# The polar factor of a scan matrix: 20 iterations inside an expert layer instead of 32 inside the attention

## What is computed

```python
x = x + attention(layernorm(x), Wq, bq, Wk, bk, Wv, bv, Wo, bo)
x = x + experts(layernorm(x), Wg, w1, w2)
x = x + scan_block(layernorm(x), W_up, W_v, W_proj, identity, W_scan_raw)
x = x + experts(layernorm(x), Wg, w1, w2)

# inside scan_block: the matrix W of the scan is the polar factor of W_scan_raw (128 x 128)
U, _, Vt = jnp.linalg.svd(W_scan_raw, full_matrices=False)
W = U @ Vt
```

## Time and profile before

| | us |
|---|---|
| three runs | 2096.91, 2099.97, 2100.51 |
| median | 2099.97 |
| the profiled execution | 2098.23 |
| its span | 2096.5 |

### The profile page before, as it was taken

The page is one execution under the profiler, slowest core; times in us unless marked ns, Lnnn a source line. Parts: engine busy times, 40 slices in busy tenths (PEclk is TensorE's granted clock), DMA queues, the critical chain, the costliest instruction groups (busy, mean ns, idle before and its releaser), DMA issues. The chain is left out here.

```text
span 2096.5 us, 44156 instructions
## 1 busy us (share of the span) xinstructions
PE 1715.4 (82%) x14662; PEld 1126.9 (54%) x14662; DVE 1421.2 (68%) x2559; ACT 970.7 (46%) x2157; POOL 688.0 (33%) x498
## 2 busy tenths in 40 slices
PE   5699989998998999899974565899999999994374
PEld 3234333333333433334344554888888888884373
DVE  7777777777787777777624125688888888884222
ACT  4166666776676677676632112233333333332120
POOL 5300000000000000000013432677777777763532
PEclk9599999999999999999965786999999999997587
DMA  3200000000000000000007215122222222212523
GB/s 109 77 17 18 17 11 17 18 17 11 18 17 11 18 17 17 11 17 18 2 21 245 72 46 147 31 81 80 80 80 80 80 80 80 80 50 82 192 69 101
DMA packets 171652, 117.20 MB, mean 56 GB/s; under 512 B 10940, under 2 KB 161852, under 8 KB 171208
## 3 DMA queue, kind: packets, MB, share of 16 engines
q1 hardware_dynamic: 167368, 106.33, 17.3%
q0 software_dynamic: 4096, 8.46, 1.1%
HBM read 63.98 MB, written 50.72 MB: 55 GB/s over the span
## 5 line engine op out<-in xcount | busy, mean ns | idle before, releaser
L557 DVE TENSOR_REDUCE chunk_max<-ps_max 128x1 f32<-128x512 f32 (+3 forms) x1280 | 698.5, 603 | 211.2 <-PE ps_max L663 123.3
L606 ACT ACTIVATE probs<-ps_s 128x512 f32<-128x512 f32 (+3 forms) x1280 | 599.6, 547 | 317.2 <-PE ps_s L655 163.8
L636 PE MATMUL ps_s<-Qs,Ks 50*128 50x512 bf16 (+3 forms) x1280 | 379.3, 357 | 70.7 <-DVE chunk_max L557 50.7
L646 PE MATMUL ps_max<-Ks,Qs 48*128 48x512 bf16 (+3 forms) x1280 | 385.8, 360 | 13.1 <-POOL a_ident L499 10.5
L706 PE MATMUL ps_o<-probs,Vp 128*32 128x512 f32 (+3 forms) x2560 | 349.9, 571 | 11.4 <-ACT O_sb L589 11.1
L514 POOL TENSOR_TENSOR A_b<-A_newton,b_tile 128x128 f32<-128x128 f32 x32 | 14.6, 455 | 917.5 <-ACT A_newton L613 917.5
L1424 POOL TENSOR_TENSOR lane_products<-L,q 128x1024 f32<-128x1024 f32 x132 | 309.5, 2376 | 4.0 <-DMA L<-scanned 4.0
L636 PEld LDWEIGHTS ps_s<-Qs,Ks 50*128 50x128 bf16 x1280 | 103.1, 94 | 311.2 <-DVE chunk_max L557 247.1
L1479 DVE TENSOR_TENSOR weighted<-exp_scores,psV_s 128x4096 f32<-128x4096 f32 x44 | 194.2, 4413 | 0.2 <-issue 0.2
L1437 POOL TENSOR_TENSOR q<-L,z_normed 128x1024 f32<-128x1024 f32 x44 | 141.6, 3218 | 144.7 <-DVE z_normed L1459 144.7
L1558 PE MATMUL psS<-ident,lane_products 128*128 128x128 f32 x1408 | 169.4, 279 | 23.7 <-POOL lane_products L1424 23.7
(11 more groups left out here) (224 smaller groups left out, 2375.0 us busy)
## 6 DMA issues: line engine op xcount, KB each, us to landing
scanned<-q SPq DMA_DIRECT2D x44, 512.0 KB
L<-scanned SPq DMA_DIRECT2D x44, 512.0 KB
m_w<-in_L_ffn_w_dram SPq DMA_DIRECT2D x32, 512.0 KB
Qs<-q_parts SPq DMA_DIRECT2D x192, 32.0 KB
Ks<-k_parts SPq DMA_DIRECT2D x192, 32.0 KB
dispatched<-m_blank SPq DMA_DIRECT2D x2, 2080.0 KB
m_blank<-dispatched SPq DMA_DIRECT2D x16, 260.0 KB
routed<-m_blank SPq DMA_DIRECT2D x2, 2048.0 KB
```

The costliest lines, as they stand in the source:

```text
L557: nc.vector.tensor_reduce(out, scores[:, 0:w], axis=AX.X, op=ALU.max).then_inc(max_reduced, 1)
L606: nc.scalar.activation(dst, ps_s[(k + r) % R][:, q0:], ACT.Exp, scale=SCALE).then_inc(exp_done, 1)
L636: last = nc.tensor.matmul(ps_s[(k + r) % R][:, q0:], K[r][rows, kt * P:(kt + 1) * P], Q[r][rows, g * QW + q0:(g + 1) * QW], start=True, st ...
L646: last = nc.tensor.matmul(ps_max[(k + r) % R][:, 0:w], Q[r][rows, i * P:(i + 1) * P], K[r][rows, ck * QW:ck * QW + w], start=True, stop=no ...
```

## The change

The iteration leaves `attend` altogether: its products, copies and POOL operations, its six tiles, `newton` and two semaphores. `reads` loses the entries "A", "Y" and "X", and the waits that named them name the neighbouring entries. POOL's fill loses `b_tile` and `a_ident`.

`moe` gets an argument `polar`, true for "m0" alone. There 20 iterations run as one chain: 16 with the coefficients SPREAD and 4 with SETTLE (the coefficients used so far). PE runs them between `count(1)` and `turn(0)`, DVE behind `route(1)`, ACT behind `copy_totals(1)`. A and A A lie in the two banks of `psH[0]`, the new S and its transpose in those of `psH[1]`. DVE copies A, makes Z and Y and copies S; ACT copies the transpose. POOL makes the two scaled identities ahead of its `iota` into the blank rows.

```diff
-NEWTON = (15 / 8, -10 / 8, 3 / 8)
+SPREAD = (3.4445, -4.7750, 2.0315)
+SETTLE = (15 / 8, -10 / 8, 3 / 8)
+POLAR = [SPREAD] * 16 + [SETTLE] * 4
...
 (attend, POOL)
-            nc.gpsimd.memset(b_tile[:], NEWTON[1])
-            nc.gpsimd.tensor_scalar(a_ident[:], c.ident[:], NEWTON[0], None, ALU.mult).then_inc(made, 1)
...
-                if exp:
-                    pool.wait_ge(misc_read, reads(s, "A") + 1)
-                    nc.gpsimd.tensor_tensor(A_b[:], A[:], b_tile[:], ALU.mult).then_inc(newton_pool, 1)
-                    pool.wait_ge(newton_pool, s * 2 + 1)
-                    nc.gpsimd.tensor_tensor(Z[:], A_b[:], a_ident[:], ALU.add).then_inc(newton_pool, 1)
...
 (attend, DVE)
-                    if k == 15 and exp:
-                        newton(s)
...
 (attend, ACT)
-                    if n == 1:
-                        act.wait_ge(newton_mm, s * 3 + 1)
-                        nc.scalar.activation(A[:], newton_ps[:, 0:D], ACT.Copy).then_inc(misc_read, 1)
...
-                    if n == 6:
-                        act.wait_ge(newton_mm, s * 3 + 3)
-                        nc.scalar.activation(c.S[:].rearrange("p a d -> p (a d)"), newton_ps, ACT.Copy)\
-                          .then_inc(misc_read, 1)
...
 (attend, PE)
-                if n == 1:
-                    misc("A")
-                    nc.tensor.matmul(newton_ps[:, 0:D], c.S[:, 0, :], c.S[:, 0, :], start=True, stop=True)\
-                      .then_inc(newton_mm, 1)
...
                 if n == 3:
-                    misc("Y")
+                    misc("rows0" if nxt else "end")
                     combine(s, 0)
-                    nc.tensor.matmul(newton_ps[:, 0:D], A[:], A[:], start=True, stop=True).then_inc(newton_mm, 1)
...
-                if n == 6:
-                    nc.tensor.matmul(newton_ps[:, 0:D], c.S[:, 1, :], Y[:], start=True, stop=True)
-                    nc.tensor.matmul(newton_ps[:, D:], Y[:], c.S[:, 1, :], start=True, stop=True).then_inc(newton_mm, 1)
...
 (moe, POOL)
+            if polar:
+                for steps, t in scaled_ident.items():
+                    nc.gpsimd.tensor_scalar(t[:], c.ident[:], steps[0], None, ALU.mult).then_inc(polar_made, 1)
...
 (moe, DVE, behind route(1))
+            for i, (a, b, a2) in enumerate(POLAR if polar else []):
+                dve.wait_ge(A_in_psum, i + 1)
+                nc.vector.tensor_copy(A[:], ps_A).then_inc(A_read, 1)
+                nc.vector.scalar_tensor_tensor(out=Z[:], in0=ps_A, scalar=b, in1=scaled_ident[a, b, a2][:], op0=ALU.mult,
+                                               op1=ALU.add).then_inc(A_read, 1)
+                dve.wait_ge(AA_in_psum, i + 1)
+                dve.wait_ge(A_read, 2 * i + 2)
+                nc.vector.scalar_tensor_tensor(out=Y[:], in0=ps_AA, scalar=a2, in1=Z[:], op0=ALU.mult, op1=ALU.add)\
+                  .then_inc(Y_done, 1)
+                dve.wait_ge(X_in_psum, 2 * i + 1)
+                nc.vector.tensor_copy(c.S[:, 0, :], ps_X).then_inc(S_copied, 1)
...
 (moe, ACT, behind copy_totals(1))
+            for i in range(len(POLAR) if polar else 0):
+                act.wait_ge(X_in_psum, 2 * i + 2)
+                nc.scalar.activation(c.S[:, 1, :], ps_XT, ACT.Copy).then_inc(ST_copied, 1)
...
 (moe, PE, behind count(1), ahead of turn(0))
+            if polar:
+                pe.wait_ge(xsT_copied, NCH)
+                for i in range(len(POLAR)):
+                    if i:
+                        pe.wait_ge(S_copied, i)
+                    nc.tensor.matmul(ps_A, c.S[:, 0, :], c.S[:, 0, :], start=True, stop=True).then_inc(A_in_psum, 1)
+                    pe.wait_ge(A_read, 2 * i + 1)
+                    nc.tensor.matmul(ps_AA, A[:], A[:], start=True, stop=True).then_inc(AA_in_psum, 1)
+                    pe.wait_ge(Y_done, i + 1)
+                    if i:
+                        pe.wait_ge(ST_copied, i)
+                    nc.tensor.matmul(ps_X, c.S[:, 1, :], Y[:], start=True, stop=True).then_inc(X_in_psum, 1)
+                    nc.tensor.matmul(ps_XT, Y[:], c.S[:, 1, :], start=True, stop=True).then_inc(X_in_psum, 1)
+                pe.wait_ge(S_copied, len(POLAR))
+                pe.wait_ge(ST_copied, len(POLAR))
```

More of the change, by code:

```diff
@@ L354, in attend @@
     AHEAD = 16 * NS
-    FILLED, MADE = 2 * R + 2, 3 * R + 3
+    FILLED, MADE = 2 * R + 2, 3 * R + 2
     FIRST_MAXES = 12
@@ L381, in attend @@
         ones_row = sb("ones_row", [2, T], bf16)
-        A = sb("A_newton", [P, D])
-        A_b = sb("A_b", [P, D])
-        Z = sb("Z_newton", [P, D])
-        Y = sb("Y_newton", [P, D])
-        a_ident = sb("a_ident", [P, D])
-        b_tile = sb("b_tile", [P, D])
         ps_max = [ps(f"ps_max{u}") for u in range(R)]
@@ L435, in reads @@
             if not isinstance(s, int) or s > 0:
-                order = ["rows1", "A", "comb", "Y", "rows0", "X", "end"]
+                order = ["rows1", "comb", "rows0", "end"]
                 if not nxt:
                     order.remove("rows0")
-                return s * 6 + order.index(name)
-            return ["rows0 of head 0", "rows1", "A", "Y", "rows0", "X", "end"].index(name) if s == 0 else 0
+                return s * 3 + order.index(name)
+            return ["rows0 of head 0", "rows1", "rows0", "end"].index(name) if s == 0 else 0
         @block.sync
@@ L497, in _ @@
                 nc.gpsimd.memset(t[:, :, HD:HD + 1], 1.0).then_inc(made, 1)
-            nc.gpsimd.memset(b_tile[:], NEWTON[1])
-            nc.gpsimd.tensor_scalar(a_ident[:], c.ident[:], NEWTON[0], None, ALU.mult).then_inc(made, 1)
-            pool.wait_ge(made, n + R + 1)
-            assert (n, n + R + 1) == (FILLED, MADE)
+            pool.wait_ge(made, n + R)
+            assert (n, n + R) == (FILLED, MADE)
             nc.gpsimd.tensor_tensor(c.X[:], c.X[:], c.bo_rows[:].unsqueeze(1).broadcast_to([P, NT, D]), ALU.add)
@@ L542, in normalise @@
                   .then_inc(misc_read, 1)
-            def newton(s):
-                dve.wait_ge(newton_mm, s * 3 + 2)
-                dve.wait_ge(newton_pool, s * 2 + 2)
-                nc.vector.scalar_tensor_tensor(out=Y[:], in0=newton_ps[:, 0:D], scalar=NEWTON[2], in1=Z[:],
-                                               op0=ALU.mult, op1=ALU.add).then_inc(misc_read, 1)
             def section(s, j, r, p, exp, nxt):
@@ L757, in between @@
                 if n == 5:
-                    misc("X")
+                    misc("end")
                     combine(s, 1)
-                if n == 6:
-                    nc.tensor.matmul(newton_ps[:, 0:D], c.S[:, 1, :], Y[:], start=True, stop=True)
-                    nc.tensor.matmul(newton_ps[:, D:], Y[:], c.S[:, 1, :], start=True, stop=True).then_inc(newton_mm, 1)
                 if n == 8:
@@ L836, with moe @@
 ROW = D + 2
-def moe(nc, c, name, Wg, w1, w2, dispatched, routed):
+def moe(nc, c, name, Wg, w1, w2, dispatched, routed, polar):
     J = NT
@@ L892, in moe @@
         psY = [ps(f"psY{u}", [P, 512]) for u in range(2)]
+        if polar:
+            A, Y, Z = (sb(n, [P, D]) for n in ("A_polar", "Y_polar", "Z_polar"))
+            scaled_ident = {steps: sb(f"ident_{n}", [P, D]) for steps, n in ((SPREAD, "spread"), (SETTLE, "settle"))}
+            ps_A, ps_AA = psH[0][:, 0:D], psH[0][:, 512:512 + D]
+            ps_X, ps_XT = psH[1][:, 0:D], psH[1][:, 512:512 + D]
         logits = [t[:, 0:JH * E_].rearrange("p (j e) -> p j e", e=E_) for t in psY]
@@ L905, in moe @@
         y_sent = [sem(f"y_sent{u}") for u in range(2)]
+        polar_made, A_in_psum, A_read, AA_in_psum, Y_done, X_in_psum, S_copied, ST_copied = (
+            sem(n) for n in ("polar_made", "A_in_psum", "A_read", "AA_in_psum", "Y_done", "X_in_psum", "S_copied",
+                             "ST_copied"))
         block = cx.enter_context(nc.Block())
@@ L1029, in _ @@
             route(1)
+            if polar:
+                dve.wait_ge(polar_made, 2)
+            for i, (a, b, a2) in enumerate(POLAR if polar else []):
[9 more added lines that the diff above has]
+                nc.vector.tensor_copy(c.S[:, 0, :], ps_X).then_inc(S_copied, 1)
             for e in range(E_):
@@ L1720, in hybrid_layer @@
             project_out(nc, c)
-        moe(nc, c, "m0", Wg, w1, w2, dispatched[0], routed[0])
+        moe(nc, c, "m0", Wg, w1, w2, dispatched[0], routed[0], True)
         with ExitStack() as cx_scan:
```

5 lines of the change are left out of this document (2 added, 3 removed).

## The result

The change made the kernel slower by a third of a per cent, on the chip on which it was first timed: 2104.78 us median of 20 runs (2101.40 to 2107.14) against 2097.89 for 20 runs of the kernel before (2088.19 to 2101.59), a ratio of 1.0033 with a 95% interval of 1.0023 to 1.0042. The forecast was 2089. The profiled execution took 2103.74, span 2102.0, against 2098.23 and 2096.5.

A forecast was written before the change was run, and what follows sets the result against it. No engine is full throughout; PE and DVE bound the attention in turn, PE's chain the first expert layer. 2098.2 less 47 plus 36 gave 2087, 2089 as median; range 2066 to 2108.

The forecast's parts named there:

- The attention: Heads without the iteration: 1.45 us gained in each of 31 heads, 47 us in all, range 37 to 59.
- Everywhere else it reads back to back: Attention: outside gaps of 0.70, 1.54 and 0.67 us in each head, DVE reads without idling.
- The price of an iteration: First expert layer's chain: 3.53 us an iteration at clock 0.50, 70.6 for 20, delaying the experts 36 us.
- From a DVE result to PE's load 0.05, from PE's end to DVE 0.04: Chain in the first expert layer: us for each hand-over between DVE and PE, counted three times an iteration.
- Rival 4: Chain beside the scatter: DVE's copies are held, 6.5 us lost, 2096; chance 0.05.
- Rival 1: Chain: PE's clock rises to full, 2.63 us an iteration, delay 18, kernel at 2067; chance 0.12.
- Rival 2: Attention: the closed gap's gain is taken by the next wait, a head gains only 0.81 us, 2108; chance 0.14.
- Rival 3: Attention: with fewer products PE's clock falls within heads, 2135, or 2105 if in a third of them; chance 0.09.
- The sum: Whole kernel: 2098.2 - 47 + 36 = 2087 for the profiled execution, 2089 for the median.
- Two bounds: Upper gain of 1.84 us a head if A·A counts in full; low end 2076 from 57 gained and 36 delay.

The follow-up runs named there:

- e8: The change plus two unused identity transposes on PE behind product A and two behind A·A in every iteration, on chip A: 2093.25 us.
- e11: The change with its chain started some 11 us later by 24 ACT copies, still beside the scatter, on chip B: 2115.10 us against 2099.85 before.
- e15: The changed kernel unaltered, run again on chip C: 2085.85 us against 2097.15 for the kernel before, ratio 0.9940.
- e13: The kernel before with iterations in only 20 of 32 heads and none in the expert layer, on chip C: 2083.27 us, ratio 0.9942.

## Why the prediction was wrong

- **The attention, right.** Predicted per head: 0.41, 0.15, 0.25 and 0.64, together 1.45, heads 28.1 apart, gaps of 0.29, about 1.4 and under 0.1. Measured: 0.42, 0.17, some 0.20 and 0.67, and 0.11 at a fourth gap (1.14 to 1.03) that I hadn't priced; together 1.57, heads 27.98 apart. The fourth gap and a fifth of 1.28, which stayed, stand in every head of the kernel before, so the prediction's "Everywhere else it reads back to back" is a misreading, worth 0.11 a head. The attention ends 50.5 us earlier instead of 47: 46.9 up to the last maximum (45.0 predicted), 0.5 at the start, as predicted, and 3.2 in the last head instead of 1.6. The last part is chance, as the last head took 31.1 to 44.5 us in other executions without iterations in the heads (last section).
- **The price of an iteration, right.** 3.53 predicted, 3.54 measured; the product 0.80, the granted clock 0.50 behind the first product, as the values taken said. On chip C the experts start 70.2 behind the slots, predicted 70.
- **The step that failed: "From a DVE result to PE's load 0.05, from PE's end to DVE 0.04".** The second of these holds on chip C, and elsewhere outside the scatter. On the chip of the result PE's end reached DVE up to 7.3 us late beside the scatter, and ACT up to 8.3; two iterations lost 20.5 us by it. On A and B it was alike. I took the price from rows before the attention and in the last head, where no scatter runs. In the kernel before PE is idle in all but the first 4 us of the scatter, so no row of it could show the exchange between PE and the others there; it should have been bounded by its own uncertainty, and it had none.
- **Rival 4** looked at the scatter, but at the wrong engine. DVE's copies kept 0.29 beside it, on every chip. The rule of the Trainium skill that gave it (SBUF — State Buffer, section SBUF: two separate sides) is of an exclusive lock on the port pair that DVE shares with GpSimd. The trace shows no DVE operation of the chain held by it; all of them read PSUM.
- **Rival 1** didn't come by itself, but its price was exact (2.62 in e8). **Rival 2** didn't come: the gap of 0.67 was closed and stayed closed. **Rival 3** neither: the clock fell only where the kernel before has it fall too, four times at the loop's ends, though for 24 us together instead of 17.
- **The sum.** With 20.5 for the late results 2087 + 20.5 = 2107.5 for the profiled execution, which took 2103.7; the attention gave 3.5 more than predicted. Without them, on chip C, 2085.85 was measured, 2089 predicted. The direction was wrong on the chip of the result and on A and B, for this one term, and right on C. Two bounds don't come out of their terms, without effect on the outcome: 1.45 with A·A's 0.42 in full is 1.87 a head and not 1.84, and 57 and 36 give 2079 and not 2076.

## What to carry to other kernels

A stage in which an engine idles in the profile doesn't show how fast that engine would exchange results with the others there: work that is moved under somebody else's DMA traffic needs its hand-over priced as an unknown, above all if it is a chain of dependent steps (60 hand-overs each way here). Put only as much there as hides even if it is slowed, and leave the rest where each costs little: of 20 steps 10 still left 21 us exposed on chip A, while 5 hid on chip C and weren't run on the others. And if the difference is a few tenths of a per cent, time the kernel on several chips: here the sign of the result depended on the chip. All of this is from recorded executions; whether the hand-over is as slow without recording is open.

## What was not expected of the hardware

- **Chips differ.** The kernel before took 2094.8 to 2100.1 in its medians on chips A, B and C; the change took 2104.4, 2107.8 and 2085.9.
- **Late results of PE beside an indirect scatter.** On chips A and B a result of PE was seen by DVE up to 8.7 us late (e11) and by ACT up to 9.0 (e8), while POOL issued a scatter of 128 rows every 1.26 us; PE saw DVE's results within 0.06 all the time. Each chain beside the scatter lost 14 to 24 us.
- **A whole attention's end hangs on the clock of its last head.** There the granted clock falls at different times. Two executions of the same program, the kernel after and e15:

```profile
1000.00:1010.00 10.00, 9.55 (x49) 3.83 (x49) 0.00 (x0) 5.92 (x13) 0.00 (x0) 0.59 0.01 2
1010.00:1020.00 10.00, 10.00 (x36) 2.64 (x32) 0.00 (x0) 4.77 (x10) 0.00 (x0) 0.50 0.00 0
```

```profile
1000.00:1010.00 10.00, 9.04 (x63) 3.14 (x63) 0.00 (x0) 8.19 (x18) 0.00 (x0) 1.00 0.01 2
1010.00:1020.00 10.00, 8.75 (x49) 2.88 (x47) 0.00 (x0) 4.73 (x10) 0.00 (x0) 0.65 0.00 0
```

  The attention ends at 1028.7 in the first, at 1022.6 in the second; over all profiled executions without iterations in the heads between 1018.8 and 1033.1. All but 2 us of that lies in the last head: the last maximum is over between 987.2 and 989.0 in each of them, and the rest takes 31.1 to 44.5. The runs of single kernels spread as widely (2072.68 to 2085.71 in e13), which would fit; only one execution of each has a trace.
